# TensorE's batch loop of a fused attention and expert kernel starts at slot 0 of an instruction fetch block

## The reference

```python
content   = einsum('bqhd,bkhd->bhqk', q + u_bias, k)
pos_score = rel_shift(einsum('bqhd,khd->bhqk', q + v_bias, p))
attn      = softmax((content + pos_score) / sqrt(128))
x = x + einsum('bhqk,bkhd->bqhd', attn, v).reshape(b, s, e) @ Wo + bo
...
mask = top 2 of 8 of softmax(gelu(norm(x @ Wr1 + br1)) @ Wr2 + br2), made to sum to 1
x = x + sum over e of mask[e] * ((x1 * gelu(x2)) @ W2[e] + b2[e]),  x1, x2 = split(norm(x) @ W1[e] + b1[e])
```

## Time and profile before

| what | us |
|---|---|
| median of 3 runs | 1840.25 |
| the three runs | 1836.13, 1840.25, 1841.25 |
| the profiled execution's own time | 1836.0 |
| its span in the trace | 1834.4 |
| PE busy, matmuls (12530) | 1622.4 (88%) |
| DVE busy | 1451.7 (79%) |
| POOL busy | 1142.1 (62%) |
| ACT busy | 1089.7 (59%) |

### The profile page before, as it was taken

How to read it: one execution, slowest core, us unless ns; L and a number is a source line. 1 busy time by engine, 2 the same in 40 slices (tenths; PEclk the granted TensorE clock), 3 DMA queues, 4 the chain that set the end, 5 groups by cost and what they waited for, 6 DMA issues and landing times. The chain is left out here.

```text
span 1834.4 us, 50577 instructions
## 1 busy us (share of the span) xinstructions
PE 1622.4 (88%) x12530; PEld 1266.5 (69%) x12531; DVE 1451.7 (79%) x5423; ACT 1089.7 (59%) x2139; POOL 1142.1 (62%) x2139
## 2 busy tenths in 40 slices
PE   2699999999999999999999999999952699999997
PEld 1466766767676676766677676666731599999997
DVE  3579989978897887988798798889954477777775
ACT  2156666656666665766666575666620466666665
POOL 4168658738755873874686487478562266665665
PEclk8589999989998998999999899999975799999999
DMA  5436533733543463364355346336443133333333
GB/s 163 153 93 154 136 93 111 180 100 93 144 120 93 118 169 87 99 151 109 92 153 138 82 122 154 102 84 176 100 148 116 40 51 52 50 51 51 52 48 45
DMA packets 140445, 195.94 MB, mean 107 GB/s; under 512 B 27976, under 2 KB 102616, under 8 KB 140192
## 3 DMA queue, kind: packets, MB, share of 16 engines
q1 hardware_dynamic: 92608, 130.86, 25.7%
q0 software_dynamic: 47584, 62.19, 17.3%
HBM read 108.24 MB, written 75.27 MB: 100 GB/s over the span
## 5 line engine op out<-in xcount | busy, mean ns | idle before, releaser
L1004 DVE CUSTOM_DVE_ANT_0 junk<-pA,lmask 128x512 bf16<-128x512 f32 x1056 | 694.4, 683 | 163.0 <-PE pA L614 79.0
L917 ACT ACTIVATE prob<-pB 128x512 f32<-128x512 f32 x384 | 229.3, 597 | 231.5 <-PE pB L637 127.2
L1483 POOL DMA_INDIRECT out<-yb,dst x144 | 232.7, 1616 | 162.0 <-ACT yb L1557 85.7
L614 PE MATMUL pA<-K,QL 96*128 96x512 f32 (+3 forms) x792 | 291.3, 370 | 3.6 <-DMA K<-split_operands 2.7
L637 PE MATMUL pB<-QL,K 97*128 97x512 f32 (+3 forms) x768 | 291.3, 379 | 0.0
L635 PE MATMUL pB<-QU,K 97*128 97x512 f32 (+3 forms) x640 | 271.1, 424 | 1.1
L616 PE MATMUL pA<-K,QU 96*128 96x512 f32 (+3 forms) x660 | 241.8, 367 | 11.9 <-DVE acc L1004 11.3
L919 ACT ACTIVATE prob<-pB 128x512 f32<-128x512 f32 x384 | 228.0, 594 | 6.9 <-PE pB L637 6.5
L653 PE MATMUL pC<-prob,vext 128*32 128x256 f32 x3088 | 226.8, 398 | 0.0
L519 POOL TENSOR_TENSOR prob<-prob,upper_diag 128x128 f32<-128x128 f32 x384 | 182.6, 476 | 32.0
L472 POOL DMA_INDIRECT routed_rows<-rows_r,idx x159 | 160.6, 1010 | 50.1 <-issue 27.7
(11 more groups left out here) (305 smaller groups left out, 3765.1 us busy)
## 6 DMA issues: line engine op xcount, KB each, us to landing
QL<-split_operands SPq DMA_DIRECT2D x67, 256.0 KB, 3.5
QU<-split_operands SPq DMA_DIRECT2D x67, 256.0 KB, 3.9
K<-split_operands SPq DMA_DIRECT2D x67, 256.0 KB, 4.2
xg<-routed_rows SPq DMA_DIRECT2D x76, 132.0 KB
QL<-split_operands SPq DMA_DIRECT2D x67, 128.0 KB, 3.3
QU<-split_operands SPq DMA_DIRECT2D x67, 128.0 KB, 3.8
K<-split_operands SPq DMA_DIRECT2D x67, 128.0 KB, 3.8
split_operands<-c_h POOLq DMA_DIRECT2D x16, 512.0 KB, 6.5
```

The source lines that it names most:

```text
L614: mm = pe.matmul(dst[:, 0:low], QL[0:KROWS, s, q], K[0:KROWS, s, k0:k0 + low], start=True, stop=True)
L917: act.activation(p[:, 0:HALF], pB[:, 0:HALF], ACT.Exp, scale=SCALE).then_inc(p_exp, 1)
L1004: v.tensor_tensor_reduce(junk[:, n % S1_BUFS, :], pA[n % S1_BUFS][:, :], lmask[:, at:at + HALF], 1.0, -3.0e38, ALU.add, ALU.max, acc[:, s, ...
L1483: po.indirect_dma_start(dram["out"], bass.IndirectOffsetOnAxis(dst[k][:, a:a + 1], 0), yb[k][:, a, :], None, compute_op=ALU.add).then_inc( ...
```

## The change

```diff
-def batches(nc, eng):
+def batches(nc, eng, head=None):
 
-    return nc.Fori(0, B, engines=[eng.engine], hint_back_edge=True)
+    return nc.Fori(0, B, engines=[eng.engine], hint_back_edge=True, head_slot=None if head is None else {eng.engine: head})
...
-            with batches(nc, pe) as b:
+            with batches(nc, pe, 0) as b:
```

## The result

The changed kernel takes 1795.47 us (median of 6 runs, 1792.13 to 1804.66); the kernel before takes 1839.93 us (6 runs, 1836.13 to 1841.25). The ratio is 0.9767, with a 95% interval of 0.9742 to 0.9792: 44 us faster. The direction and the mechanism were forecast, but not the size: 26 us were forecast, and the range ended at 1800 us.

A forecast was written before the change was run, and what follows sets the result against it. PE was taken to bound the batch loop, stopping 2.4 us at each branch back. Gains of 13.2 (branch) and 18 (clock), capped at 28 by DVE, less 1.2 (exit), taken as 26, gave 1814 us; range 1800 to 1830.

The forecast's parts named there:

- What the branch waits for: PE's branch back at L768 waits for the rest of a fetch asked for on entering its block; 2.4 us.
- Item 1: At PE's seven branches back, 2420 ns becomes 0.1 to 0.2 us; gain 13.2 us of idle time before L641.
- Item 2: Behind the seven branches, 30 us at half clock go, at 0.6 us lost for each; gain 18 us.
- Item 3: DVE must follow PE; its free time around the branches allows 28 us of the 31 us gain.
- Item 4: At the batch loop's entry, the alignment, filled slots and one more branch hide behind a DMA wait; zero.
- Item 5: At the loop's exit, PE may wait for the next block in `project_out`; up to 2.4 us lost, 1.2 taken.
- Item 6: The expert loop's code moves by less than a block and still needs no fetches in its trips; zero.
- That the hint does nothing: Rival at PE's branch back: no change, because the hint or the place does not matter; chance 0.09.
- That the block comes too early and is lost: Rival at PE's branch back: block given up before the branch, which pays a whole fetch; 1863 us, chance 0.07.
- That the clock takes part of the gain back: Rival in the batch loop: DVE or the clock takes most back; gain 6 to 18 us, 1827 us, chance 0.18.

The follow-up runs named there:

- slot 64: The change with PE's loop head at slot 64 of its instruction block in place of 0; 1801.25 us, ratio 0.9728.
- slot 65: The change with PE's loop head at slot 65 of its instruction block in place of 0; 1843.42 us, ratio 1.0011 to the kernel before.
- slot 130: The change with PE's loop head at slot 130 of its instruction block in place of 0; 1838.55 us, ratio 0.9989.
- slot 160: The change with PE's loop head at slot 160 of its instruction block in place of 0; 1798.07 us, ratio 0.9769.
- 40 waits: The change with 40 waits, on a semaphore that has long had its value, added at the end of PE's trip; 1839.91 us, ratio 0.999.
- the last run: The change with small piece context 6 (L599) one unit later on PE, and its copy one later on DVE; 1780.34 us, ratio 0.9683.
- 30 waits: The change with 30 waits, on a semaphore that has long had its value, added at the end of PE's trip; 1840.53 us, ratio 1.0006.
- 20 waits: The change with 20 waits, on a semaphore that has long had its value, added at the end of PE's trip; 1808.06 us, ratio 0.9809.

## Why the prediction was right and wrong

**What the branch waits for: right.** The branch waits for the rest of a fetch that was asked for at the last block boundary; slots 64 and 65, one slot apart, give 0.36 and 3.7 us (means). The kernel before had about 1.0 us of lead, and 3.4 to 3.5 less that is its 2.4 us. One detail was missing: at slots 130 and 160 the request left later than the count of instructions said, it seems because of waits near the boundary.

**Item 1, the branch time: right.** The 13.2 us of idle time went. The branch takes 0.35 us and not 0.1 to 0.2, and queued matmuls cover it. The trip fetches 11 blocks (94 in all, 92 or so forecast), and the packet starts 7.3 to 9.2 us ahead, not 10 or more.

**Item 2, the clock: this is the step that failed.** The mechanism was right, but I looked for it in too narrow a place. I counted only the 30 us at half clock behind the seven branches, and priced them at 0.6. The time at half clock fell by twice that, by 61.4 us. The trips without their first 7 us show it, one of before and one of after:

```profile
732.60:880.30 147.70, 140.69 (x1105) 102.98 (x1108) 129.62 (x526) 96.93 (x184) 101.74 (x232) 0.95 0.46 119
```

```profile
412.00:553.80 141.80, 134.81 (x1098) 98.80 (x1100) 127.91 (x521) 95.45 (x182) 101.06 (x230) 0.99 0.48 124
```

In these inner parts the time at half clock was 81.9 us before, 24 stretches of 3.4 (one of 6.8 counts as two), and is 51.2 now, 15 of them. Behind the heads it was 30.7 and is 0. The price was lower than mine: PE's busy time fell by 28.0 us, 0.46 for each of the 61.4. With the 2.5 us of idle time that went besides the stop it is 30.5 us, 0.50. In the prediction the inner stretches were a reserve for the range's lower end only: three fewer, 6 us. It was nine fewer, 30.7 us. With these counted, at the 0.50 found since, the sum is 13.2 + 30.5, the 43.7 us measured. That the inner stretches would follow the stops was not in my working. The run with 40 waits has them back without a late fetch; how a stop brings them on is open.

**Item 3, DVE's cover: wrong.** I capped the gain at 28 us by DVE's free time around the heads alone. But DVE waited for PE all through the trip, and those waits (L1004 and L1010) fell from 138.8 to 99.1 us in the loop. The gain passed the cap by 16 us. Right was only that DVE is next: in the last run its L616 wait takes back part of the gain.

**Item 4, the entry: right**, zero: PE is idle 3.17 us ahead of the first L641 as before. **Item 5, the exit: wrong but small.** It costs nothing in place of 1.2 us. The next block's packet starts 1.1 us after the branch that is not taken, and `project_out` has no gap in it:

```profile
1316.16 3.35 PE L686 MATMUL pA<-w_o,t 128*128 128x128 f32 x16
1333.09 1.09 PE L694 MATMUL pE<-ident_f,rows_r 128*128 128x128 f32 x4 [13.58 <-DVE rows_r L1077]
```

**Item 6, the expert loop: right**, zero: no packet of q8 moves in its trips, before (1490 to 1820 us) or after (1450 to 1775).

**The rivals.** That the hint does nothing was refuted by the run without it, where the branch has a median of 3.5 us. That the block comes too early and is lost did not happen: its packet starts up to 9.2 us ahead of the branch, and the branch is short. That the clock takes part of the gain back had the wrong sign.

**What stays open.** In the runs with 30 waits, at 65 and without the hint, nearly every trip is 157.0 us long, whatever the stop. The table shows what gives way: from 30 waits to slot 65 the stops grow by 11.2 us, PE's other idle time falls by 7.9 and its busy time by 3.5. Why these add up to the same length was not tried. Nor was it tried where between 0.87 and 1.47 us of idle time the step lies. Nor does the number of half clock stretches follow from the idle times alone: the run at slot 64 has 68.3 us at half clock and the change 51.2, with 44.5 and 44.4 us idle. The runs of the change differ by 12 us, and the longest run has the lowest granted clock of them (0.932 at 1804.7 us, 0.937 at 1792.1).

## What to carry to other kernels

Where each trip of a loop fetches its code again (11 or 12 blocks here), look at the closing branch in the sequencer's rows. Here it took 0.34 to 0.48 us where its block had been asked for in time (0.73 in one trip at slot 160) and 1.9 to 4.1 where it had not. Being in time took both a branch hint and a last block boundary far enough ahead: some 3.5 us between the request and the branch. At slot 130 the request left 1.5 us ahead where the count of instructions said 3.3, it seems because of a wait near the boundary. One slot of the head's place, 64 or 65, made 42 us, so the slot is worth fixing once the body's length is known.

The stops of the array here cost more through the clock than by their length: without their 13.2 us of idle time 61.4 us less were spent at half clock, half of them (30.7) outside the first 7 us behind the stops, and PE was busy 28.0 us less. So compare PE's busy time for the same number of matmuls before you put a stall down at its own length. One idle time of 1.45 us in each trip, taken out of TensorE's stream by moving a small piece, was worth 15 us of 1795 here.

## What the hardware showed that I had not expected

- A request for code became a packet after 0.9 to 1.1 us (once 1.5), and the branch went on 3.4 to 4.1 us after the request (the fourteen taken branches at slot 65 and without the hint, if the request leaves as the branch starts). The branch stopped for the whole of it at slot 65, and took 0.36 us where it lay 255 instructions behind the boundary, at slot 64.
- The loss is a step in the idle time of each trip: 0.87 us (20 waits) cost about 12 us in all, 1.47 us (30 waits) cost 45, and 3.1 us (slot 65) only 3 more.
- Taking the stops out also took out nine of the 24 half clock stretches far from them. The 1.45 us wait near the end of each trip stayed, and is followed by half clock in four of seven trips, where it had been in all seven.
